# An attention and expert block: scores turned onto block-diagonal queries, value eviction and value bias moved

## The reference

```
mod = silu(c) @ wmod -> sa, ca, ga, sb, cb, gb    (per batch, 128 each)
ga, gb: sign kept, size at least 0.25
h = layernorm(x) * (1 + ca) + sa
q, k, v = h @ WQ.T + bq, h @ WK.T + bk, h @ WV.T + bv   (16 heads of 8)
q, k = rope(q), rope(k)
attn = softmax(causal(q k.T / sqrt(8))) v
x = x + ga * (attn @ Wo.T + bo)
h = layernorm(x) * (1 + cb) + sb
the 2 best of 8 experts by router logits, softmax of the two as shares
x = x + gb * sum(share * (gelu(h @ w_fc + b_fc) @ w_proj + b_proj))
```

## Time and profile before

| | us |
|---|---|
| median of 3 runs (lowest to highest) | 586.28 (584.28 to 586.44) |
| the profiled execution | 582.33 |
| its span, first to last instruction | 580.5 |
| busy PE, PEld | 474.6, 382.3 |
| busy DVE, ACT, POOL | 401.2, 306.9, 344.6 |

### The profile page before, as it was taken

One profiled execution on the slowest core, in us unless ns is written; L12 is line 12 of the kernel. 1 busy time (PEld: TensorE's weight loads), 2 busy tenths in 40 slices (PEclk: granted clock), 3 DMA queues, 4 the chain that ended last, 5 costly groups with the idle time before them and its releaser, 6 DMA issues.

```text
span 580.5 us, 13494 instructions
## 1 busy us (share of the span) xinstructions
PE 474.6 (82%) x3982; PEld 382.3 (66%) x3982; DVE 401.2 (69%) x1200; ACT 306.9 (53%) x878; POOL 344.6 (59%) x476
## 2 busy tenths in 40 slices
PE   2478889779779797887887887887999999999950
PEld 1346566556557565565565565566899999999940
DVE  6676788797896888888888969752455554446642
ACT  1014555445554544554554545554678788788740
POOL 5514354455863963873873864762487677556762
PEclk9879999999997999999999999986999999999995
DMA  5223522723623435435336354311123233235622
GB/s 143 75 64 103 139 79 71 208 79 106 188 79 107 135 109 140 119 110 155 105 107 165 86 113 128 90 34 48 47 73 80 77 102 98 73 89 168 193 55 99
DMA packets 71894, 61.53 MB, mean 106 GB/s; under 512 B 10329, under 2 KB 65245, under 8 KB 71824
## 3 DMA queue, kind: packets, MB, share of 16 engines
q1 hardware_dynamic: 65712, 51.15, 32.2%
q0 software_dynamic: 4544, 8.47, 4.4%
q10 hardware_dynamic: 1568, 1.05, 0.7%
HBM read 26.45 MB, written 13.04 MB: 68 GB/s over the span
## 4 chain that ended last, share of the span: by engine, by line
PE 58%; DVE 18%; issue 8%; ACT 4%; DMA 4%; POOL 3%; SPq 2%; ACTq 1%; DVEq 0%; POOLq 0%
PE ps_sc L1424 10%; PE ps_pv L1544 6%; PE ps_max L1432 6%; PE ps_pv L1432 5%; PE misc L1588 5%; DVE maxima L1246 4%; DVE z L939 3%; PE ps_sc L1517 3%; PE misc L1559 3%; PE misc L1526 2%; DVE low L1204 2%; PE ps_max L1492 2%; PE ps_max L1485 2%; PE ps_max L1487 2%; PE misc L1580 2%
## 5 line engine op out<-in xcount | busy, mean ns | idle before, releaser
L841 ACT ACTIVATE probs<-ps_sc 128x512 f32<-128x512 f32 x192 | 114.9, 599 | 118.7 <-PE ps_sc L1517 66.7
L1246 DVE TENSOR_REDUCE maxima<-ps_max 128x2 f32<-128x512 f32 (+1 forms) x192 | 131.3, 684 | 57.3 <-PE ps_max L1494 39.7
L708 POOL TENSOR_SCALAR_AFFINE_SELECT probs<-probs 128x512 f32<-128x512 f32 x128 | 81.9, 640 | 76.2 <-ACT probs L841 75.0
L695 POOL DMA_INDIRECT results<-after_k,row_in x78 | 77.8, 997 | 54.0 <-DVE after_k L1020 38.1
L805 ACT ACTIVATE after_k<-ps_sc,after_k 128x128 f32<-128x128 f32 x312 | 98.4, 374 | 0.3 <-PE ps_sc L1424 0.3
L1424 PE MATMUL ps_sc<-x_in,after_k 128*128 128x128 f32 x624 | 84.8, 280 | 2.5 <-DVE after_k L1013 2.2
L1424 PEld LDWEIGHTS ps_sc<-x_in,after_k 128*128 128x128 f32 x624 | 77.5, 195 | 3.3 <-issue 2.4
L655 POOL DMA_INDIRECT sorted_rows<-rows,slots x64 | 64.6, 1010 | 14.5 <-issue 7.5
L1513 PE MATMUL ps_sc<-q_stacks,k_diags 128*128 128x256 f32 x256 | 62.9, 328 | 1.3 <-DMA q_stacks<-shift_t 1.3
L1492 PE MATMUL ps_max<-k_diags,q_stacks 128*128 128x512 f32 x128 | 62.1, 485 | 1.7 <-DVE maxima L1246 1.7
L1013 DVE COPY after_k<-wfc_s 128x644 f32 x78 | 40.6, 520 | 30.2 <-issue 30.0
(11 more groups left out here) (157 smaller groups left out, 930.5 us busy)
## 6 DMA issues: line engine op xcount, KB each, us to landing
k_diags<-k_stack SPq DMA_DIRECT2D x64, 128.0 KB
gate_now<-gate_rows SPq DMA_DIRECT2D x16, 320.0 KB, 4.2
row_in<-sorted_rows SPq DMA_DIRECT2D x78, 65.0 KB, 1.8
k_stack<-high SPq DMA_DIRECT2D x32, 128.0 KB, 2.1
q_stacks<-high SPq DMA_DIRECT2D x32, 128.0 KB
x_in<-in_x SPq DMA_DIRECT2D x16, 128.0 KB, 3.0
k_stack<-low SPq DMA_DIRECT2D x16, 128.0 KB, 2.1
q_stacks<-low SPq DMA_DIRECT2D x16, 128.0 KB
```

Source lines behind the costliest of these rows:

```text
L695: nc.gpsimd.indirect_dma_start(result_dram, bass.IndirectOffsetOnAxis(ap=row_in[m % RING][:, D + 1:D + 2].bitcast(U32), axis=0), y_out[m % ...
L708: nc.gpsimd.affine_select(four, four, [[0, 4], [1, P]], ALU.is_ge, 0.0, base=0, channel_multiplier=-1).then_inc(S["causal_done"], 1)
L841: nc.scalar.activation(probs[:, g % 2, c], ps_sc[u % 2][:], ACT.Exp, scale=SCALE).then_inc(S["exp_done"], 1)
L1246: nc.vector.tensor_reduce(to, of, AX, ALU.max).then_inc(S["max_done"], 1)
```

## The change

- Scores are turned: `q_stack` is spread by four more DMAs per step onto a block diagonal `q_diag` (two buffers), and one matmul per unit has the keys of `k_stack` (now three buffers) for all four heads as weights and 512 columns of `q_diag` moving. Units are now (keys 0, queries 0), (keys 1, queries 1), (keys 0, queries 1), so POOL selects in the first two, and the weighing waits for the third exponential itself. The shift DMA writes into `q_diag`, in 2 partitions instead of 8, and waits for its spread. The zero rows go.
- The values are copied out by ACT, without bias, at n=10. The value bias is transposed, multiplied by `wo` and added to the output bias before that is multiplied by the gate, once.
- `normalise` of batch t+2 goes from slot 7 to 6. `heads_out` goes to the front of its slot on ACT.
- `roped` and `row_scaled` go: POOL works in place in `turned_a` and `rows`. Several small tensors are laid over others. `gates` is loaded behind the last scores and not in step 3. POOL clears the new buffers: two of `k_stacks` and `q_diags[0]` in step -1, `q_diags[1]` in step 0.

```diff
-NORMALISE_NEXT_AT = 7
+NORMALISE_NEXT_AT = 6
-STACKED = 16 * 4
+STACKED = 16 * 3
...
 def stack_k():
-    s.wait(sp, S["k_spread"], 0, SPREAD, SPREAD)
+    s.wait(sp, S["score_mm"], -2, UNITS, UNITS)
...
 def stack_q_high():
-    s.wait(sp, S["score_mm"], -1, UNITS, UNITS)
+    s.wait(sp, S["max_mm"], -1, UNITS, UNITS)
+    s.wait(sp, S["q_spread"], -1, SPREAD, SPREAD)
...
-    sp.dma_start(shift_rows_of(q), zero_row[:]...broadcast_to([8, GROUPS, T])).then_inc(S["stacked"], 16)
...
+def spread_q():
+    if s.has(1):
+        s.wait(sp, S["stacked"], 1, STACKED, STACKED)
+        s.wait(sp, S["score_mm"], -1, UNITS, UNITS)
...
+        for w in range(4):
+            at = slice(ROWS * w, ROWS * (w + 1))
+            sp.dma_start(q_diag[(s.t + 1) % 2][at, :, w, :].bitcast(F32), q_stack[(s.t + 1) % 2][at].bitcast(F32)
+                         ).then_inc(S["q_spread"], 16)
...
 stack_k(); stack_q_high(); spread_k(); stack_q_low()
+spread_q()
...
 def clear_rest():
...
+    nc.gpsimd.memset(k_stacks[:, 1:3].bitcast(F32), 0.0).then_inc(S["zeroed"], 1)
+    for g in range(GROUPS):
+        nc.gpsimd.memset(q_diags[:, 0, g].bitcast(F32), 0.0).then_inc(S["zeroed"], 1)
...
+def clear_second():
+    for g in range(GROUPS):
+        nc.gpsimd.memset(q_diags[:, 1, g].bitcast(F32), 0.0).then_inc(S["zeroed"], 1)
...
 def keep_causal(g, m, d):
-    s.wait(pool, S["exp_done"], d, UNITS, 3 * g + 2 + m)
+    s.wait(pool, S["exp_done"], d, UNITS, 3 * g + 1 + m)
...
+def values_out():
+    s.wait(act_e, S["v_mm"], 1, 1, 1)
+    s.wait(act_e, S["pv_mm"], -1, 4, 4)
...
+    nc.scalar.activation(v_wide[(s.t + 1) % 2][:, :, :, 0:DK], misc[BANK["v"]][:, 0:T]..., ACT.Copy).then_inc(S["v_done"], 1)
...
 def shift_out(g, d):
-    act_e.dma_start(shift_rows_of(q_stack[(s.t + d) % 2])[:, g, :], shift_t[g % 2][:].bitcast(F32))...
+    s.wait(act_e, S["q_spread"], d, SPREAD, SPREAD)
+    act_e.dma_start(shift_rows_of(q_diag[(s.t + d) % 2])[0:2, g], shift_t[g % 2][:].bitcast(F32))...
...
 for n in range(UNITS):                       # ACT
+    if n in HEADS_OUT_AT and s.has(HEADS_OUT_AT[n][1]):
+        heads_out(*HEADS_OUT_AT[n])
+    if n == 10 and s.has(1):
+        values_out()
     outs = ...                               # shift_out, then exp
-    if n in HEADS_OUT_AT and s.has(HEADS_OUT_AT[n][1]):
-        heads_out(*HEADS_OUT_AT[n])
...
+dve.wait_ge(S["bias_tr"], 1)                 # gates_and_masks
+nc.vector.tensor_copy(bias_v, ps_max[0][:, 0:B]).then_inc(S["bias_turned"], 1)
+dve.wait_ge(S["bias_mm"], 1)
+nc.vector.tensor_tensor(bias_o, ps_max[0][0:B, D:2 * D], bo_s[0:B], ALU.add).then_inc(S["bias_added"], 1)
...
 def scores(u, d):
-    if c < 2:
-        for n in range(2):
-            last = nc.tensor.matmul(bank[:, n * T:(n + 1) * T], ks[:, g, 2 * c + n, 0:P], q[:, g, :], ...)
-    else:
-        for w in range(4):
-            last = nc.tensor.matmul(bank[:, w * P:(w + 1) * P], ks[:, g, w, P:T], q[:, g, P:T], ...)
+    keys, late = ((0, 0), (1, 1), (0, 1))[c]
+    last = nc.tensor.matmul(ps_sc[u % 2][:].rearrange("p (w q) -> p w q", w=4),
+                            k_stack[(s.t + d) % 3][:, g, keys * P:(keys + 1) * P],
+                            q_diag[(s.t + d) % 2][:, g, :, late * P:(late + 1) * P], start=True, stop=True)
...
 def weigh(g, d):
+    s.wait(pe, S["exp_done"], d, UNITS, 3 * g + 3)
...
+nc.tensor.transpose(ps_max[0][:, 0:P], bqkv_s[:, 2 * D:3 * D], ident_s[:]).then_inc(S["bias_tr"], 1)
+nc.tensor.matmul(ps_max[0][0:B, D:2 * D], bias_v, wo_s[:], start=True, stop=True).then_inc(S["bias_mm"], 1)
```

More of the change, by code:

```diff
@@ L275, in block_program @@
         k_diag = [k_diags[:, n] for n in range(2)]
-        k_stack = sb("k_stack", [P, GROUPS, T], F32R)
-        zero_row = sb("zero_row", [8, T], F32R)
+        k_stacks = sb("k_stacks", [P, 3, GROUPS, T], F32R)
+        k_stack = [k_stacks[:, n] for n in range(3)]
+        with nc.sbuf_tensor("q_diags", [P, 2, GROUPS, 4, T], F32R) as q_diags:
+            pass
+        after_e = sb("after_e", [P, 2 * GROUPS * 4 * T])
+        q_diag = [q_diags[:, n] for n in range(2)]
         maxima = sb("maxima", [P, TILES, HEADS])
@@ L500, in stack_k @@
                         s.wait(sp, S["low_done"], 1, 2, 1)
-                        s.wait(sp, S["k_spread"], 0, SPREAD, SPREAD)
+                        s.wait(sp, S["score_mm"], -2, UNITS, UNITS)
+                        if s.t == 0:
+                            sp.wait_ge(S["zeroed"], 14)
                         for n, part in enumerate((high, low, high)):
-                            sp.dma_start(way(k_stack, n), part[:, 1, :].bitcast(F32)).then_inc(S["k_stacked"], 16)
+                            sp.dma_start(way(k_stack[(s.t + 1) % 3], n), part[:, 1, :].bitcast(F32)).then_inc(S["k_stacked"], 16)
                 def stack_q_high():
@@ L618, in _ @@
         def _(pool):
-            for t, v in ((half_s[:], -0.5), (k_stack[:].bitcast(F32), 0.0), (rows[:].rearrange("p n r -> p (n r)")[0:8, 0:GROUPS * T], 1.0),
-                         (zero_row[:].bitcast(F32), 0.0), (q_stacks[:].bitcast(F32), 0.0)):
+            for t, v in ((half_s[:], -0.5), (k_stack[0].bitcast(F32), 0.0), (rows[:].rearrange("p n r -> p (n r)")[0:8, 0:GROUPS * T], 1.0),
+                         (q_stacks[:].bitcast(F32), 0.0)):
                 nc.gpsimd.memset(t, v).then_inc(S["zeroed"], 1)
-            pool.wait_ge(S["zeroed"], 5)
+            pool.wait_ge(S["zeroed"], 4)
             def clear_rest():
@@ L728, in emit @@
                         clear_rest()
+                    if n == 5 and s.t == 0:
+                        clear_second()
                     if n == 8 and s.has(-1):
@@ L1334, in emit @@
                                               misc[BANK["router"]][:, 0:TILES * EXPERTS]).then_inc(S["logits_done"], 1)
-                    if n == 10 and s.has(1):
-                        values()
                     if n == NORMALISE_NEXT_AT and s.has(2):
@@ L1545, in weigh @@
                                 ps_pv[ROWS * w:ROWS * (w + 1), a * P:T], vw[:, a, 4 * g + w, :],
-                                both[:, w, :] if a == 0 else later[:, w, :],
+                                both[:, w] if a == 0 else later[:, w, :],
                                 start=(a == 0), stop=(a == 1), skip_group_check=True)
```

137 lines of the change are left out of this document (71 added, 66 removed).

## The result

| | before | after |
|---|---|---|
| median of the compared runs, us | 585.28 (583.78 to 586.44, 4 runs) | 562.91 (561.03 to 563.37, 4 runs) |
| the profiled execution, and its span | 582.33, 580.5 | 563.05, 561.3 |
| mean granted clock | 0.953 | 0.949 |

The ratio after to before is 0.9613, 95% interval 0.9578 to 0.9648: 22.4 us gained, where 27 were forecast (559, range 546 to 577). Medians are of all runs; the ratios leave out executions that fell into a slower state, so a ratio can differ a little from the quotient of two medians.

The account below looks back on a forecast made before the run. No engine is full, so hand-overs set a step. Step gains of 31 us, less 2 for traffic and 2 for start, give 27: 555.3 us profiled, 559 on the median's scale, range 546 to 577.

Parts of the forecast that it names:

- the terms: Attention steps: gains of z, heads_out and scores sum to 2.8 us with search and z, 1.8 with z alone.
- the 4 us booked for traffic and start: Deducted from the 31 us gain: 2 us for new DMAs meeting shift DMAs, 2 for memsets at the start.
- z, 1.6 and 0.65 a step: Normalising at n=6: PE's wait for z shrinks, gaining 1.6 us in steps with search, 0.65 in odd steps.
- Scores, 0.32 a step: One 512-column matmul per unit saves 0.16 us each at n=0 and n=3, where PE is the chain.
- heads_out, 0.86 a step: ACT's copy at the front of its slot finds its input ready; PE's wait for heads_t goes, 0.86 us a step.
- Values, nothing: Value copy moved from DVE to ACT: DVE loses 0.41 us, ACT's idle time hides the copy; nothing booked.
- Selects, nothing: POOL's selects one unit earlier: same instructions at earlier or equal times; nothing booked.
- Stacks and spreads, SP's chain: SP's chain to q_low stays covered by 1 us; rival that it replaces removed waits: 575 to 577 us, 15%.
- The cover: q_low expected landed at 245.7, next step's start at 246.7: SP's chain covered by 1 us only.
- Start, 2 us: POOL's clearing of new buffers at the start costs 2 us, with bounds of -1.4 and +9.
- the rival on memsets: GpSimd's memsets block VectorE at the start, costing all 9 us and not 2: 566 us; chance 10%.
- A step of 20.3 us with DVE at 18.4: Forecast step length after the change, with DVE busy 18.4 us and PE 18.0 of it.

Follow-up runs that it names:

- half maxima: The changed kernel with each VectorE maximum taken over half of the keys, 256 instead of 512 columns: 546.01 us, ratio 0.9386 to the kernel before.
- the two orders alone: The kernel before with only heads_out at the front of its slot and the batch after next normalised in slot 6: 573.31 us, ratio 0.9854.

## Why the prediction was right, and where it was not

- **Sign, size, mechanism.** Right: hand-overs set the step, and heads_t and z were the ones that fell. Forecast 27 us, measured 22.4. The twelve steps gave 17.7 us where the terms gave 26.6 (five of 2.8, seven of 1.8): 1.8 and 1.2 a step on the mean, and 1.7 and 1.0 in the two steps shown. That the total came so near owes something to luck: 8.9 us missing in the steps and 3.7 lost behind them stand against the 4 us booked for traffic and start, which were not needed.
- **z, 1.6 and 0.65 a step: the term that was mis-sized most.** I took z's 0.59 us from its old neighbours. At the new place it takes 1.29 (odd step 0.96) beside POOL, on the chain of waits. The 0.70 and 0.37 missing are most of the shortfall of 1.1 and 0.8 in the two steps shown. That is a subtraction and no experiment: no run kept z at its place and made it short, and with z in slot 3, where it took 0.67 in most odd steps, they were no shorter. As a part it was worth more than I said: undone alone it costs 3.2 us an even step and 0.3 an odd one, because the wait it removes would by now cost granted clock as well.
- **Scores, 0.32 a step.** I held that PE is the chain at n=0 and n=3. In the changed kernel the chain at n=0 is VectorE's, and the narrow matmuls cost 0.18 us in the odd steps and nothing that shows in the even ones: half of the term or less.
- **heads_out, 0.86 a step.** The wait went in each step. Put back alone it costs 0.49; its full size shows only in the stretch behind the rank matmul. So the parts, undone one by one, do not add up to the whole, and the shortfall can't be divided among them exactly.
- **Values, nothing:** right within 0.05 us a step. **Selects, nothing:** right in sum, wrong in the rows: the shift beside them is stretched by 0.7 us, which costs 0.29 in each odd step and nothing that shows in the even ones.
- **Stacks and spreads, SP's chain.** The cover was 1 us by my count. The low queries were late in three of twelve steps, by 1.4 us at most and 2.5 in all: near the edge, on the safe side. Doubling the spreads cost nothing that shows.
- **Start, 2 us:** nothing. The bias and casts did come onto the path, as the rival on memsets had it (mask_b 1.98 us), but behind cover of the same length.
- **Left out:** `gates` moved into the last scatters. I had named the move and not priced it, against my own rule on moved transfers. It stretches a wait of POOL by 2.7 us; what it costs of the 3.7 us lost at the end is not shown.
- **A step of 20.3 us with DVE at 18.4** was called tight, but possible. DVE is busy 19.1 to 19.4, since its instructions stretch beside POOL's, and steps last 20.8 or more. DVE is the fullest engine, but it alone is not shown to be the floor: with half maxima and with z in slot 3 PE ends up waiting for POOL's select in the odd steps.

What stays open: which part carries the 0.3 us a step between the two orders alone and the whole change, why that run's times and its profile differ on the share of the two orders, and what the stretch behind t=15 loses its clock to.

## What to carry to other kernels

An instruction that is moved is priced by its new neighbours on the engine that shares its port, not by its old row. Once hand-overs are shortened, ask which engines are left near the step's length: work taken off one comes back in part as a wait, here 0.4 us off PE for 0.2 in the odd steps and about 3.5 off VectorE for 1.2. Where a pipeline has two kinds of steps, read them apart: their mean hid a gain of 0.29 us in one kind. And a wait of PE can cost more than its length, where the granted clock falls behind it, as behind 3.15 us here.

## What the hardware did that I had not expected

Idle times of TensorE of the same length did not always have the same answer in the granted clock. In the kernel before, a wait for z of 2.35 us in the step of the earlier trace rows left it at 1.00, and so did three more of 2.35 and 2.36 us in other even steps, but one of 2.36 us did not. From the timeline of PE and the windows of before:

```profile
173.32 0.44 PE L1573 MATMUL misc<-ident_s,z 128*128 128x128 f32 x2 [2.36 <-DVE z L939]
```

```profile
174.00:176.00 2.00, 2.00 (x16) 1.28 (x19) 1.33 (x6) 0.72 (x2) 0.06 (x1) 0.68 0.84 217
176.00:178.00 2.00, 2.00 (x24) 1.59 (x16) 0.00 (x0) 0.33 (x1) 1.26 (x2) 0.50 0.81 238
```

That step lasted 24.37 us, 1.5 more than its like. Behind waits of 3.14 to 3.16 us (z in slot 7) the mean clock was below 1.00 in all five even steps. With z in slot 3 it also fell, behind two shorter waits close together, 1.68 and 1.14 us: over 205 to 211 us PE was busy 3.18 of 6. In the changed kernel the clock was 1.00 in all twelve steps of t=2 to 13. So part of what the change won there is clock not lost, some 2 us by the lengths of t=6 and 7 before, though over the whole span the mean clock is no higher (0.949 for 0.953): behind t=15 more was lost. A wait's price is its length only as long as the clock stays.
